# A router's layer norm with mean times deviation as a second operand from PSUM, interleaved with the next group's statistics

## The chip, the cores and the metric

One core of one Trainium2 chip. The metric is the device time of one execution in microseconds (us). Before the change three runs took 1918.94 us in the median (1918.43 to 1921.91).

## The reference, cut to what matters

The kernel computes a block of three layers on 8192 rows of 256 float32 values: `x = x + 0.5 * moe(norm(x))`, then `x = x + attention(norm(x))`, then `x = x + 0.5 * moe(norm(x))`. The change touches the norm in front of the two expert networks:

```python
def _layernorm(x, axis=-1, eps=1e-05):
    m = jnp.mean(x, axis=axis, keepdims=True)
    v = jnp.var(x, axis=axis, keepdims=True)
    return (x - m) / jnp.sqrt(v + eps)
```

Each expert network takes the normed rows, computes `logits = xf @ router_w.T` for 8 experts, a softmax, the top two of each row, and a list of at most 1280 rows for each expert; then every expert runs its rows through three matrices.

## The kernel before, in words

The 8192 rows are 64 tiles of 128 rows. All of x stays in SBUF (`xs`). Every expert network begins with a stage that this text calls **the norm stage** (`ffn_in` on each engine). It takes the tiles in 16 groups of four (G4 = 4); two groups are a pair, and 8 pairs are the 8 steps (STEPS = 8). Group q = 2i + r belongs to step i and to buffer r (0 or 1). Buffers `xn`, `rows`, `rstd`, `bst` and `mv` exist twice, once for each r.

For one group the work passes through the engines in this order:

- VectorE, `stats` (lines 920 to 930): four `bn_stats` (L924), four `bn_aggr` that write mean and variance into PSUM (`mv`, L928), and one small instruction that adds epsilon (L930). It releases `stat_ready`.
- GpSimd, `power` (L418): the power -1/2 of four numbers for each partition, giving `rstd`, which is one over the deviation. It releases `rstd_ready`.
- VectorE, `norm` (L937): four `tensor_scalar`, (x - mean) * rstd, each 128x256 float32 from SBUF to SBUF, with the two numbers for each partition as pointers (mean in PSUM, rstd in SBUF). It waits for `lo_ready` (the buffer of two groups ago is done with) and `rstd_ready`.
- ScalarE, `high` (L667): the upper float16 half of all four tiles into `rows`. It waits for the store of two groups ago and for `xn_ready`.
- GpSimd, `low` (L422): the lower half, `xn - high`, a `tensor_tensor` with two SBUF inputs and an SBUF output.
- TensorE transposes `rows` (L1346) into PSUM, ScalarE copies the result out (`turned`, L673), TensorE multiplies with the router's weights (L1357), and after every second group ScalarE takes the logits out (L677). SyncE stores `rows` to memory for the experts' gathers (L515) and, in the first network, loads the next pair of x (L518).

The engines' orders are written by hand. VectorE's before is, in step i: stats(i, 1), norm(i, 0), stats(i+1, 0), norm(i, 1). GpSimd's is power(2i+1), low(2i), power(2i+2), low(2i+1). ScalarE's is high(i, 0), the copies of the group before, the logits, high(i, 1), the copies. SyncE waits for the pair's load before, loads the next pair and then stores the two groups of this pair. Between the pieces of VectorE's order stands `beside(n)`, a hook. In the first network it holds three small router pieces (n = 0, 1, 2). In the second it holds the last work of the attention (`attention_end`): at n = 1 a residual sum (`finish`, L1198), at 4 to 10 a chain that builds the last batch's matrix together with TensorE and ScalarE (`m2_sums`, `m2_ctx`, `m2_out` L1240, `m2_top` L1247, `m2_scale` L250, `m2_lo`), and at 14, 16, 18, 20 four more residual sums. `ffn_in` runs some steps unrolled (1 in the first network, 5 in the second) and the others in a hardware loop. After the norm stage VectorE goes on with `top_two` (L971 to L996), GpSimd with constants, and the routing rounds follow.

Of the kernel before, what the change touches and what calls it, by code (L numbers as in the profile page):

```python
# [6 lines left out]
def macaron_block(nc, x, wq, bq, wv, bv, wo, bo, router_w, wg, wu, wd, out):  # L7
# [3 lines left out]
    add, sub, mult = ALU.add, ALU.subtract, ALU.mult  # L11


    P = 128
    B, SEQ, D = x.shape
# [17 lines left out]
    G4 = 4  # L33
    PAIR = 2 * G4
    STEPS = NT // PAIR
# [17 lines left out]
    with ctx:  # L53
        def sb(name, shape, dt):
            return ctx.enter_context(nc.sbuf_tensor(name, shape, dt))
# [4 lines left out]
        bank = [ctx.enter_context(nc.psum_tensor(f"bank{i}", [P, 512], f32)) for i in range(8)]  # L60
# [8 lines left out]
        xs = sb("xs", [P, NT, D], f32)  # L69
# [6 lines left out]
        xn = sb("xn", [P, 2, G4, D], f32)  # L76
        xt2 = sb("xt2", [P, 2, 2, 2 * KD, P], f16)
        bst = sb("bst", [P, 2, G4, 6], f32)
        mv = bank[1][:, 256:256 + 4 * G4].rearrange("p (r g s) -> p r g s", r=2, g=G4)
        rstd = sb("rstd", [P, 2, G4], f32)  # L80
        nmean = sb("nmean", [P, 2, G4], f32)
        ident16 = sb("ident16", [P, P], f16)
# [161 lines left out]
        def settle(eng):  # L244

            eng.sem_inc(s_passed, 1)
# [44 lines left out]
        def tiles(ap, t, n):  # L291

            return ap[:, t:t + n] if isinstance(t, int) else ap[:, bass.ds(t, n)]
# [554 lines left out]
        def _(dve):  # L848
# [69 lines left out]
            def ffn_in(S, ch, wait_x, head, beside):  # L918
                def stats(i, r):

                    t = i * PAIR + r * G4
                    wait_x(i, r)
                    for g in range(G4):
                        ch.mark(dve.bn_stats(bst[:, r, g, :], tiles(xs, t + g, 1)[:, 0]))  # L924
                    ch.wait()
                    settle(dve)
                    for g in range(G4):
                        ch.mark(dve.bn_aggr(mv[:, r, g, :], bst[:, r, g, :]))  # L928
                    ch.wait()
                    dve.tensor_scalar(rstd[:, r, :], mv[:, r, :, 1], EPS, XSCALE ** -2, add, mult).then_inc(S.stat_ready, 1)  # L930

                def norm(i, r):
                    t, q = i * PAIR + r * G4, 2 * i + r
                    dve.wait_ge(S.lo_ready, q + 1)
                    dve.wait_ge(S.rstd_ready, q + 1)
                    for g in range(G4):
                        last = dve.tensor_scalar(xn[:, r, g, :], tiles(xs, t + g, 1)[:, 0], mv[:, r, g, 0:1],  # L937
                                                 rstd[:, r, g:g + 1], sub, mult)
                    last.then_inc(S.xn_ready, 1)

                def step(i, beside):
                    stats(i, 1)
                    beside(4 * i + 1)
                    norm(i, 0)
                    beside(4 * i + 2)
                    stats(i + 1, 0)
                    beside(4 * i + 3)
                    norm(i, 1)
                    beside(4 * i + 4)

                stats(0, 0)
                beside(0)
                for i in range(head):
                    step(i, beside)
                with dve.Fori(head, STEPS - 1) as i:
                    ch.enter(i - head, 2 * 2 * G4)
                    step(i, nothing)
                    ch.leave(STEPS - 1 - head)
                stats(STEPS - 1, 1)
                norm(STEPS - 1, 0)  # L960
                norm(STEPS - 1, 1)

            def route(S, ch):

# [179 lines left out]
            def ffn(S, wait_x, head, beside):  # L1144
                ch = Chain(dve, S.dstep)
                ffn_in(S, ch, wait_x, head, beside)
                route(S, ch)
                for i in range(LP):
                    list_piece(S, 0, i)
                list_read(S, ch, 0)  # L1150
                for k in range(4):
                    dve.wait_ge(S.gu_hi, k + 1)
                    split_lo(k % 2, k // 2, S.gu_lo)
                with dve.Fori(0, E - 1) as e:
                    ch.enter(e, 3 + 1 + 3 + (0 if S.scaled else 12 + 4))
                    expert(S, ch, e, False)
                    ch.leave(E - 1)
                expert(S, ch, E - 1, True)

            ch = Chain(dve, at.dstep)  # L1160
# [451 lines left out]
```

## Time and profile before

| | |
|---|---|
| median of three runs | 1918.94 us |
| the profiled execution | 1917.76 us |
| its span, first to last instruction | 1916.0 us |
| TensorE busy | 1616.2 us (84% of the span) |
| VectorE busy | 1246.2 us (65%) |
| ScalarE busy | 887.6 us (46%) |
| GpSimd busy | 874.8 us (46%) |
| mean granted clock of TensorE | 0.943 |
| the norm stages | about 6 to 80 us and 1055 to 1135 us |

PE is TensorE, PEld its weight load, DVE VectorE, ACT ScalarE, POOL GpSimd, SP SyncE; a q behind the name is the engine's queue. Times count from the first instruction. In a timeline a row may hold several instructions in succession (x4): the second number is then the time from the start of the first to the end of the last. A busy share is not a bound: the norm stages use TensorE little, and what is worth something there is the chain of waits.

### The profile page before, as it was taken

How to read it: one execution, taken by the hardware profiler on the slowest of the kernel's cores; microseconds unless marked ns; L12 is line 12 of the kernel's file. 1: busy time of each engine (PE TensorE's matmuls, PEld its weight loads, DVE VectorE, ACT ScalarE, POOL GpSimd, SP SyncE). 2: the span in 40 equal slices, each digit the busy share in tenths (PEclk: the TensorE clock that was granted, in tenths of full speed). 3: DMA queues.
4: the chain of work that ended last, by engine and by line, in shares of the span. 5: the costliest groups of instructions: out<-in, count | busy, mean ns of one | idle time of the engine just before them, and what ended most of it. 6: DMA issues, size and time to landing. Idle time of an engine off the chain costs nothing.

```text
span 1916.0 us, 40317 instructions
## 1 busy us (share of the span) xinstructions
PE 1616.2 (84%) x13943; PEld 1275.8 (67%) x13943; DVE 1246.2 (65%) x2883; ACT 887.6 (46%) x1627; POOL 874.8 (46%) x636
## 2 busy tenths in 40 slices
PE   4512899999999999995899751289999999999998
PEld 3411687877878787773577641168787787878876
DVE  8987748576574856526898897763745546465551
ACT  4511445445454444535665551144544545445452
POOL 5623262644536354235776652326264452635423
PEclk9999999999999999996999755589999999999999
DMA  6650461614425152226766450045161442515212
GB/s 214 212 185 14 108 122 30 145 41 107 78 70 126 37 132 52 31 29 165 154 146 146 137 195 4 14 108 116 36 145 44 104 83 65 128 42 126 58 25 28
DMA packets 261236, 182.16 MB, mean 95 GB/s; under 512 B 160938, under 2 KB 247860, under 8 KB 261172
## 3 DMA queue, kind: packets, MB, share of 16 engines
q1 hardware_dynamic: 230452, 139.37, 26.7%
q0 software_dynamic: 30720, 41.96, 13.2%
q8 instruction: 36, 0.59, 0.1%
q14 instruction: 28, 0.23, 0.0%
HBM read 89.01 MB, written 54.53 MB: 75 GB/s over the span
## 4 chain that ended last, share of the span: by engine, by line
PE 72%; DVE 12%; issue 6%; POOL 5%; DMA 2%; ACT 2%; DVEq 0%; SPq 0%; POOLq 0%; ACTq 0%
PE bank L1439 43%; PE bank L1452 22%; PE bank L1420 3%; POOL rstd L418 1%; POOL rows L422 1%; DVE kT L1020 1%; DVE rT L1020 1%; PE bank L1400 1%; DVE gat L1229 1%; PE bank L1484 1%; ACT xn L778 1%; DMA xs<-in_L_attn_x 1%; POOL gat L395 1%; DVE xn L937 1%; DVE v L1223 1%
## 5 line engine op out<-in xcount | busy, mean ns | idle before, releaser
L1439 PE MATMUL bank<-xT,w_g 128*128 128x320 f16 x3072 | 503.1, 300 | 30.9 <-DMA xT<-gat 30.9
L1095 DVE SCALAR_TENSOR_TENSOR unit_buf<-bank,sc_cur,unit_buf 128x320 f32<-128x320 f32 x512 | 281.5, 550 | 353.9 <-PE bank L1439 227.9
L1439 PE MATMUL bank<-xT,w_u 128*128 128x320 f16 x3072 | 502.5, 300 | 0.0
L720 ACT ACTIVATE unit_buf<-bank,sc_cur 128x320 f32<-128x320 f32 x512 | 269.5, 526 | 407.1 <-PE bank L1439 405.6
L1452 PE MATMUL bank<-w_d,xs 128*128 128x256 f16 x3840 | 423.8, 273 | 0.0
L1452 PEld LDWEIGHTS bank<-w_d,xs 128*128 128x128 f16 x3840 | 375.2, 98 | 44.4
L1439 PEld LDWEIGHTS bank<-xT,w_g 128*128 128x128 f16 x3072 | 295.7, 99 | 141.0 <-issue 30.6
L389 POOL TENSOR_TENSOR hot_v<-hot_b,val 128x400 bf16<-128x400 bf16 x128 | 147.7, 1154 | 519.9 <-DVE hot_b L1078 519.9
L1439 PEld LDWEIGHTS bank<-xT,w_u 128*128 128x128 f16 x3072 | 301.3, 98 | 117.7
L1101 DVE TENSOR_TENSOR xs<-unit_buf,xs 128x320 f16<-128x320 f32 x512 | 268.0, 523 | 2.2
L395 POOL DMA_INDIRECT gat<-rows_d,id_next x160 | 177.0, 1106 | 200.4 <-DVE id_next L1088 140.0
L726 ACT ACTIVATE xs<-unit_buf 128x320 f16<-128x320 f32 x512 | 235.8, 461 | 10.4 <-DVE unit_buf L1095 10.4
L745 ACT ACTIVATE xs<-bank,w_fac 128x256 f32<-128x256 f32 x160 | 76.0, 475 | 277.4 <-PE bank L1452 276.3
L408 POOL DMA_INDIRECT out_x<-xs,id_cur x80 | 143.0, 1788 | 84.6 <-issue 76.1
L408 POOL DMA_INDIRECT x_d<-xs,id_cur x80 | 142.6, 1782 | 84.0 <-issue 73.6
L915 DVE SCALAR_TENSOR_TENSOR w_g<-raw_gu,sc_next,w_g 128x1024 f16<-128x1024 f32 x32 | 41.1, 1284 | 93.2 <-ACT w_g L661 93.2
L1420 PEld LDWEIGHTS bank<-hot_v,hot_a 128*128 128x128 bf16 x1024 | 82.3, 161 | 28.5 <-DVE hot_a L1080 24.3
L1420 PE MATMUL bank<-hot_v,hot_a 128*128 128x50 bf16 x1024 | 80.6, 219 | 22.2 <-POOL hot_v L389 22.2
L1400 PE MATMUL bank<-cnt,same_e 128*128 128x3 f32 x60 | 17.6, 363 | 95.7 <-DVE rT L1020 95.7
L422 POOL TENSOR_TENSOR rows<-xn,rows 128x1024 f16<-128x1024 f32 x32 | 68.4, 2136 | 45.2 <-ACT rows L667 45.2
L1080 DVE TENSOR_TENSOR hot_a<-pos_a,slot_a 128x1024 bf16<-128x1024 bf16 x128 | 87.3, 682 | 0.0
L1400 PEld LDWEIGHTS bank<-cnt,same_e 128*128 128x128 f32 x60 | 15.0, 310 | 98.9 <-DVE rT L1020 98.9
(229 smaller groups left out, 1815.2 us busy)
## 6 DMA issues: line engine op xcount, KB each, us to landing
rows_d<-rows SPq DMA_DIRECT2D x32, 512.0 KB, 3.4
raw_gu<-in_L_ffn_wg SPq DMA_DIRECT2D x16, 1024.0 KB, 6.3
raw_gu<-in_L_ffn_wu SPq DMA_DIRECT2D x16, 1024.0 KB, 9.3
raw_d<-in_L_ffn_wd SPq DMA_DIRECT2D x16, 1024.0 KB, 5.5
x_d<-xs SPq DMA_DIRECT2D x1, 8192.0 KB, 32.6
out_x<-xs SPq DMA_DIRECT2D x16, 512.0 KB, 3.7
xs<-in_L_attn_x SPq DMA_DIRECT2D x7, 1024.0 KB, 5.6
xs<-x_d SPq DMA_DIRECT2D x5, 1024.0 KB, 6.1
```

The costliest lines, as they stand in the source:

```text
L389: pool.tensor_tensor(hot_v[:, r], bc(hot_b[:, r], 2, 5), bc(vv, 3, ST), mult).then_inc(S.hot_v_ready, 1)
L395: pool.indirect_dma_start(out=gat[:, s, :], out_offset=None, in_=rows_d, in_offset=bass.IndirectOffsetOnAxis(ap=id_next[:, s:s + 1], axis= ...
L408: pool.indirect_dma_start(out=dst, out_offset=bass.IndirectOffsetOnAxis(ap=id_cur[:, s:s + 1], axis=0), in_=stage[:, s, :], in_offset=None ...
L422: pool.tensor_tensor(rows[:, r, :, D:2 * D], xn[:, r, :, :], rows[:, r, :, 0:D], sub).then_inc(S.lo_ready, 1)
L720: act.activation(act_s[:, u % 2, :], bank[u % 2][:, 0:CW], ACT.Silu, scale=sc_cur[:, 3:4]).then_inc(S.s_ready, 1)
L726: act.activation(hid[:, 0, f, c * CW:(c + 1) * CW], h32[:, u % HB, :], ACT.Copy).then_inc(S.hhi_ready, 1)
L1080: dve.tensor_tensor(hot_a[:, r], bc(pa, 1, P), slot_a[:, :, :], ALU.is_equal).then_inc(S.hot_a_ready, 1)
L1095: dve.scalar_tensor_tensor(h32[:, u % HB, :], bank[2 + u % 2][:, 0:CW], sc_cur[:, 4:5], act_s[:, u % 2, :], mult, mult).then_inc(S.h32_rea ...
L1101: dve.tensor_tensor(hid[:, 1, f, c * CW:(c + 1) * CW], h32[:, u % HB, :], hid[:, 0, f, c * CW:(c + 1) * CW], sub).then_inc(S.h_ready, 1)
L1420: last = pe.matmul(bank[6][:, 0:5 * ST], hot_a[:, i % 2, :, t], hot_v[:, i % 2, t].rearrange("p v s -> p (v s)"), start=(i == 0 and t == 0 ...
L1439: mm = pe.matmul(bank[2 * m + u % 2][:, 0:CW], wgu[m][:, w, k, f * P:(f + 1) * P], xT[:, a * KD + k, c * CW:(c + 1) * CW], start=(j == 0 a ...
L1452: mm = pe.matmul(bank[4 + s % 2][:, 0:D], hid[:, a, f, s * P:(s + 1) * P], wdn[:, w, f, :], start=(f == 0 and j == 0), stop=(f == FT - 1 a ...
```

## The change

The norm is now computed as x * rstd - (mean * rstd). A new small instruction (`means`) multiplies mean and rstd of a group into PSUM (`mean_r`), and `norm` is a `scalar_tensor_tensor`: in0 is the tile in SBUF, the scalar is rstd in SBUF, in1 is `mean_r` in PSUM, one number for each partition spread over 256 elements with step 0. `stats` is cut into `stats`, `moments` and `variance`, and a `turn` deals with one group: the statistics of the next group, `means` of this one, moments of the next, two tiles of the norm, variance of the next, two tiles. The hooks stand behind the turns, two after each.

```diff
--- before.py
+++ after.py
@@ -77,6 +77,7 @@
         xt2 = sb("xt2", [P, 2, 2, 2 * KD, P], f16)
         bst = sb("bst", [P, 2, G4, 6], f32)
         mv = bank[1][:, 256:256 + 4 * G4].rearrange("p (r g s) -> p r g s", r=2, g=G4)
+        mean_r = bank[1][:, 272:272 + 2 * G4].rearrange("p (r g) -> p r g", r=2)
         rstd = sb("rstd", [P, 2, G4], f32)
         nmean = sb("nmean", [P, 2, G4], f32)
         ident16 = sb("ident16", [P, P], f16)
@@ -922,43 +923,62 @@
                     wait_x(i, r)
                     for g in range(G4):
                         ch.mark(dve.bn_stats(bst[:, r, g, :], tiles(xs, t + g, 1)[:, 0]))
+
+                def moments(r):
                     ch.wait()
                     settle(dve)
                     for g in range(G4):
                         ch.mark(dve.bn_aggr(mv[:, r, g, :], bst[:, r, g, :]))
+
+                def variance(r):
                     ch.wait()
                     dve.tensor_scalar(rstd[:, r, :], mv[:, r, :, 1], EPS, XSCALE ** -2, add, mult).then_inc(S.stat_ready, 1)
 
-                def norm(i, r):
-                    t, q = i * PAIR + r * G4, 2 * i + r
-                    dve.wait_ge(S.lo_ready, q + 1)
-                    dve.wait_ge(S.rstd_ready, q + 1)
-                    for g in range(G4):
-                        last = dve.tensor_scalar(xn[:, r, g, :], tiles(xs, t + g, 1)[:, 0], mv[:, r, g, 0:1],
-                                                 rstd[:, r, g:g + 1], sub, mult)
-                    last.then_inc(S.xn_ready, 1)
+                def means(i, r):
+                    dve.wait_ge(S.rstd_ready, 2 * i + r + 1)
+                    ch.mark(dve.tensor_tensor(mean_r[:, r, :], mv[:, r, :, 0], rstd[:, r, :], mult))
+
+                def norm(i, r, tile):
+                    if tile == 0:
+                        dve.wait_ge(S.lo_ready, 2 * i + r + 1)
+                    ins = dve.scalar_tensor_tensor(xn[:, r, tile, :], tiles(xs, i * PAIR + r * G4 + tile, 1)[:, 0],
+                                                   rstd[:, r, tile:tile + 1],
+                                                   mean_r[:, r, tile:tile + 1].to_broadcast([P, D]), mult, sub)
+                    if tile == G4 - 1:
+                        ins.then_inc(S.xn_ready, 1)
+
+                def turn(i, r):
+                    n = r ^ 1
+                    stats(i + r, n)
+                    means(i, r)
+                    moments(n)
+                    norm(i, r, 0)
+                    norm(i, r, 1)
+                    variance(n)
+                    norm(i, r, 2)
+                    norm(i, r, 3)
 
                 def step(i, beside):
-                    stats(i, 1)
-                    beside(4 * i + 1)
-                    norm(i, 0)
-                    beside(4 * i + 2)
-                    stats(i + 1, 0)
-                    beside(4 * i + 3)
-                    norm(i, 1)
-                    beside(4 * i + 4)
+                    for r in range(2):
+                        turn(i, r)
+                        beside(4 * i + 2 * r + 1)
+                        beside(4 * i + 2 * r + 2)
 
                 stats(0, 0)
+                moments(0)
+                variance(0)
                 beside(0)
                 for i in range(head):
                     step(i, beside)
                 with dve.Fori(head, STEPS - 1) as i:
-                    ch.enter(i - head, 2 * 2 * G4)
+                    ch.enter(i - head, 2 * (2 * G4 + 1))
                     step(i, nothing)
                     ch.leave(STEPS - 1 - head)
-                stats(STEPS - 1, 1)
-                norm(STEPS - 1, 0)
-                norm(STEPS - 1, 1)
+                turn(STEPS - 1, 0)
+                means(STEPS - 1, 1)
+                ch.wait()
+                for tile in range(G4):
+                    norm(STEPS - 1, 1, tile)
 
             def route(S, ch):
```

## Rows read from the trace of the kernel before

**Rows 1.** The page: the chain that ended last, by engine.
```profile
PE 72%; DVE 12%; issue 6%; POOL 5%; DMA 2%; ACT 2%; DVEq 0%; SPq 0%; POOLq 0%; ACTq 0%
```

**Rows 2.** Waits, 28 to 72.5 us: waiter <- releaser, us in total, times, longest.
```profile
ACT rows L667 <- DVE xn L937: 11.0, 11, 1.5
```

**Rows 3.** Timeline, first network: start us, length us, engine, line, what, [idle before].
```profile
17.65 1.40 DVE L937 TENSOR_SCALAR xn<-xs,bank,rstd 128x256 f32<-128x256 f32 x4
...
37.96 2.13 POOL L422 TENSOR_TENSOR rows<-xn,rows 128x1024 f16<-128x1024 f32 x1 [1.12 <-ACT rows L667]
...
38.99 2.23 DVE L937 TENSOR_SCALAR xn<-xs,bank,rstd 128x256 f32 x4
...
41.14 1.39 DVE L924 BATCH_NORM_STATS2 bst<-xs 128x6 f32 x4
41.25 1.06 ACT L667 ACTIVATE rows<-xn 128x1024 f16<-128x1024 f32 x1 [1.54 <-DVE xn L937]
...
42.21 1.92 ACT L673 ACTIVATE xt<-bank 128x1024 f16<-128x1024 f16 x2
42.38 2.12 POOL L422 TENSOR_TENSOR rows<-xn,rows 128x1024 f16<-128x1024 f32 x1 [1.13 <-ACT rows L667]
42.68 0.39 DVE L928 BATCH_NORM_AGGREGATE bank<-bst 128x2 f32<-128x6 f32 x4 [0.15 <-DVE bst L924]
```

**Rows 4.** Single lines of VectorE: count, duration ns min/median/max, starts, shapes.
```profile
L937 DVE TENSOR_SCALAR xn<-xs,bank,rstd x4: 404/404/1245, 39.0 to 40.8; 128x256 f32 x4
...
L1229 DVE SCALAR_TENSOR_TENSOR gat<-gat,v x16: 1224/2006/2361, 890.6 to 1052.1; 128x1024 f32<-128x1024 f32 x16
...
L1198 DVE SCALAR_TENSOR_TENSOR xs<-bank,mx,xs x32: 732/739/752, 952.9 to 1109.7; 128x512 f32 x16, 128x512 f32<-128x512 f32 x16
...
L1240 DVE SCALAR_TENSOR_TENSOR t<-bank,zr,rT x8: 473/476/485, 939.7 to 1073.5; 128x256 f32<-128x256 f32 x8
```

**Rows 5.** Timeline of VectorE and GpSimd in the attention.
```profile
939.67 0.87 DVE L1240 SCALAR_TENSOR_TENSOR t<-bank,zr,rT 128x256 f32<-128x256 f32 x2 [1.30 <-PE bank L1533]
...
951.65 2.14 POOL L479 TENSOR_TENSOR unit_buf<-gat,unit_buf 128x1024 f16<-128x1024 f32 x1
...
952.87 1.41 DVE L1198 SCALAR_TENSOR_TENSOR xs<-bank,mx,xs 128x512 f32 x2
```

**Rows 6.** DMA issues, 14 to 80 us: count, KB each, median us to landing.
```profile
rows_d<-rows SPq DMA_DIRECT2D x14, 512.0 KB, 3.5
xs<-in_L_attn_x SPq DMA_DIRECT2D x6, 1024.0 KB, 5.6
```

**Rows 7.** Windows: stretch, length, busy us (and instructions) of each engine, clock, DMA share, GB/s.
```profile
41.30:50.10 8.80, 5.61 (x82) 4.80 (x81) 8.26 (x27) 6.04 (x8) 6.59 (x4) 1.00 0.73 237
```

**Rows 8.** Timeline, end of the first network's norm and start of its routing.
```profile
74.14 3.99 DVE L937 TENSOR_SCALAR xn<-xs,bank,rstd 128x256 f32<-128x256 f32 x8
...
76.68 1.06 ACT L667 ACTIVATE rows<-xn 128x1024 f16<-128x1024 f32 x1 [1.60 <-DVE xn L937]
...
81.48 2.12 POOL L422 TENSOR_TENSOR rows<-xn,rows 128x1024 f16<-128x1024 f32 x1 [1.36 <-ACT rows L667]
...
81.74 2.27 DVE L977 TENSOR_TENSOR t<-t,v 128x384 f32<-128x384 f32 x1
```

**Rows 9.** Timeline, norm of the second network's inputs.
```profile
1059.62 1.98 POOL L418 TENSOR_TENSOR rstd<-rstd,mhalf 128x4 f32<-128x4 f32 x2
...
1060.74 1.40 DVE L937 TENSOR_SCALAR xn<-xs,bank,rstd 128x256 f32<-128x256 f32 x4 [0.64 <-POOL rstd L418]
...
1077.41 0.28 DVE L1247 TENSOR_REDUCE m_top_s<-bank 1x1 f32<-1x128 f32 x1 [1.43 <-PE bank L1538]
...
1081.83 0.16 DVE L250 TENSOR_SCALAR mx<-bank 128x1 f32<-128x1 f32 x1 [2.10 <-PE bank L1542]
...
1109.05 1.40 DVE L1198 SCALAR_TENSOR_TENSOR xs<-bank,mx,xs 128x512 f32<-128x512 f32 x2
...
1129.27 4.00 DVE L937 TENSOR_SCALAR xn<-xs,bank,rstd 128x256 f32<-128x256 f32 x8
```

## The prediction

> **What bounds the kernel now.** I read the page's chain of waits first [rows 1]. TensorE holds 72% of it, nearly all in the experts, which the change doesn't touch. What can change lies in the two norm stages, so the chain inside these stages decides. The list of waits in the first of them shows one regular wait in front of ScalarE's `high`: 11 times, 11.0 us, on the norm [rows 2]. The timeline then shows the cycle [rows 3]. One `low` on GpSimd (L422) starts at 37.96, the next at 42.38, so a group takes 4.42 us. From the first group after the load (norm from 17.65, over at 19.05) to the end of group 14's norm at 76.68 [rows 8] it is 57.63 us for 13 groups, 4.43 each.
>
> The cycle's links can be read off in order [rows 3, 4]. A norm starts at 38.99, while `low` runs from 37.96 to 40.09. Its four instructions take 2.23 us, where the same four take 1.40 at 17.65 with no `low` beside them. The extra time lies in one instruction: 1245 ns against a median of 404, and it ends at 40.23, 0.14 after `low`. So the first `tensor_scalar` is held until `low` is over. Then come the other three (over at 41.22), `high` from 41.25 (1.06), and the next `low` from 42.38 (2.12), which holds the next norm. Norm's rest 1.13 + high 1.06 + low 2.12 + handovers 0.11 = 4.42. The cycle is closed by this hold, not by a semaphore: the norm waits only for the `low` of two groups ago.
>
> No engine is full: in 8.8 us (two groups) GpSimd works 6.59 and ScalarE 6.04, and VectorE's 8.26 hold some 1.7 us of being held [rows 7].
>
> The page "SBUF — State Buffer" of the Trainium skill, section "Who interferes with whom", says why: VectorE and GpSimd share a pair of ports, which a `tensor_scalar` from SBUF to SBUF can take whole, as can GpSimd, and the later one waits. By that rule the trace agrees (the 1245 ns).
>
> **The change part by part.**
>
> *The hold.* The new norm has one tensor in SBUF and one in PSUM. The nearest rows are L1198, also `scalar_tensor_tensor` with a PSUM tensor, an SBUF tensor and a pointer in SBUF: 32 of them lie between 732 and 752 ns, among them the pair at 952.87, right beside a GpSimd `tensor_tensor` of L422's kind (951.65 to 953.79) [rows 4, 5]. A `scalar_tensor_tensor` with both tensors in SBUF (L1229) spreads from 1224 to 2361 ns [rows 4]. So I take the hold as gone. With it the closed cycle is gone, and each engine has its own sum.
>
> *VectorE's sum for a group.* Statistics 1.39, aggregates 0.39 with 0.15 of waiting in front [rows 3]. The norm: L1240, the same instruction on 128x256 (PSUM and SBUF exchanged), takes 476 ns, and two in succession 0.87 us, so one follows the other after 0.39 [rows 4, 5]; four cost 1.57, where `tensor_scalar` costs (1.40 - 0.40)/3 = 0.33 each, 1.33. `means` isn't in the trace; it is a small operation like the variance's, and I estimate 0.16, all of it on the path, since the wait of `moments` now stands behind it too. Bounds: 0.08 (the step between two aggregates, (0.39 - 0.16)/3) and 0.32. The variance sits between two norm tiles: 0.10. Sum: 1.39 + 0.16 + 0.15 + 0.39 + 1.57 + 0.10 = 3.76; with the loop's branch I take **3.8 us** for 4.43. For the norm's step the bounds are 0.33 (today's) and 0.48 (nothing overlaps): 3.5 and 4.1 us.
>
> The page "VectorE: DVE Perf Modes" of the Trainium skill, section "The perf-mode tier table", speaks against the change: a float32 `tensor_scalar` within SBUF runs two elements a cycle, one with a PSUM operand one. By it 256 elements at 0.96 GHz would cost 0.13 us more for each tile, 0.53 a group, and the gain would be some 7 us smaller. The rows show 0.33 against 0.39, and my sum goes by them.
>
> *The other engines at 3.8 us.* GpSimd: `low` 2.12 + `power` about 1.0 (two in 1.98 [rows 9]) = 3.1. ScalarE: 1.06 + 1.92, with half a logits copy some 3.2. Both fit. Stores: `high` must wait until the store of two groups ago has landed, so two groups can't take less than `high` 1.06 + `low` 2.12 + landing 3.5 [rows 6] + handovers 0.3 = 7.0, 3.5 a group. The transfers are 0.73 busy in 8.8 us [rows 7], 6.4 us for each pair; at 7.6 us that is 0.85, so the landings may grow by half a microsecond, and the store's loop comes to about 3.75. It sits right beside VectorE's sum: SP's queue is the next in line, with a load of 5.6 us behind the stores. `power` of a group now starts behind the second norm tile, still 0.9 before the norm's end, and is over before `means` of the next turn asks for it.
>
> *First network.* Group 1 waits for its neighbour's load as before, but the new turn has the next group's moments inside: its norm ends about 0.35 later, at 19.4. Then 13 groups at 3.8 end group 14 at 68.8, against 76.68: **7.9 us**. The last two groups lose their joint norm [rows 8]: group 15 must now wait for `power`, and ends 2.7 instead of 1.5 us behind group 14. I cost this at nothing: routing's first instructions are held by `low` anyway, and L977 at 81.74 waits for the last `low` (81.48 to 83.60), whose start hangs on ScalarE's copies of group 14. If that cover is gone, it costs 1.2.
>
> *Second network.* `means` of group 0 waits for GpSimd's first `power`, which is late (1059.62) behind attention work; today only the norm waits (0.64 us at 1060.74) [rows 9]. Queued behind it are now the moments of group 1 and the residual sum L1198, which frees the PSUM bank that TensorE's chain needs. That costs about 1 us. The chain `m2_top`, `m2_scale` waits today 1.43 and 2.10 us for TensorE [rows 9]; the hooks in pairs put the first wait right behind its cause, the second behind a whole turn. I take that as even. From 1062 to the last residual sum at 1109.05 most groups aren't in the closed cycle, and I take 1 us of gain net. From there to the end of group 14 (1129.27 + 4.00 - 1.40 = 1131.87) it is 22.8 us; with 1.32 for the residual sum and five groups at 3.8, 20.3: 2.5 us. Together **3.5 us**.
>
> *Sum:* 7.9 + 3.5 = 11.4 us. The profiled execution, 1917.76, would be 1906.4; the median of the runs is 1.2 above it, so **1907.5 us**. With 3.5 us a group both terms rise to some 17 (1902); with 4.1 they fall to some 5 (1914).
>
> **The rivals.**
>
> *A new bound near the old one* (20%). The store's landing, the load, or a turn's waits hold the group at 4.15 us: 13 x 0.28 - 0.35 + 1.7 = 5 us, 1914 (1911.5 to 1916). For it: the transfers' 0.85, and a store's loop of 3.75 beside a sum of 3.76. Against it: two groups of slack in every buffer.
>
> *More than expected* (6%): norm steps at today's 0.33, and a shorter wait in the attention's chain: below 1902.
>
> *The hold remains* (6%), the case on the other side. The norm reads its pointer `rstd` from SBUF beside the tile; if this second read is held by `low` like L937's is, the cycle stays closed, and now has the dearer norm in it, 0.25, with the variance, 0.10. 4.43 becomes 4.8, over 28 groups 10 us: 1929. It decides from 4.45 us a group on. Against it stand the 32 even durations of L1198, which has such a pointer too.
>
> *The gain is swallowed* (4%): what follows the norm stage waits for something that doesn't come earlier, such as the first experts' weights or the stores. 1918. Against it: these loads are issued by SP behind the last `low`, so they move along.
>
> **How the numbers follow.** 64% for the forecast, 1902 to 1911.5. A measurement of this kernel can tell about 0.2% (3.8 us) from no change, so faster means below 1915.1. Forecast 64, high case 6 and 17 of the new bound's 20 make 0.87. Its other 3 and the swallowed 4 make 0.07, the remaining hold 0.06. The range from 1902 to 1915 holds the forecast and most of the new bound, about 8 in 10.
>
> **What would show it.** Each norm instruction at 0.47 to 0.49 us with no long one; `low` starting every 3.8 us; VectorE without gaps but for 0.15 in front of the aggregates; the end of group 14 near 68.8; the second stage shorter by 3.5. I am wrong if a norm instruction of over 1 us stays beside `low`, if ScalarE's `high` waits for the store, or if VectorE waits in `means` inside the loop.

## The result, and the profile after

The changed kernel takes 1909.69 us (median of five runs, 1907.42 to 1911.83) against 1918.94 before: a ratio of 0.9945 (0.9935 to 0.9956), 10.6 us faster by the ratio (the medians themselves differ by 9.3), where 11.4 were forecast. The profiled execution took 1911.83 us with a span of 1910.1, the slowest of the five.

On the page the chain by engine is the same as before within a percent [rows 1]:

```profile
PE 72%; DVE 12%; issue 6%; POOL 4%; DMA 2%; ACT 2%; SPq 0%; DVEq 0%; POOLq 0%; ACTq 0%
```

The new norm instruction in the whole trace (count, duration ns min/median/max, starts; it answers to L937 in [rows 4]):

```profile
L944 DVE SCALAR_TENSOR_TENSOR xn<-xs,rstd,bank x128: 444/472/480, 12.5 to 1126.9; 128x256 f32<-128x256 f32 x128
```

None of 128 is long. The hold is gone. A group of the first network that nothing hinders, on VectorE's timeline:

```profile
22.93 1.40 DVE L925 BATCH_NORM_STATS2 bst<-xs 128x6 f32 x4
...
24.25 0.15 DVE L939 TENSOR_TENSOR bank<-bank,rstd 128x4 f32<-128x4 f32 x1
24.56 0.39 DVE L931 BATCH_NORM_AGGREGATE bank<-bst 128x2 f32<-128x6 f32 x4 [0.15 <-DVE bank L939]
24.85 0.84 DVE L944 SCALAR_TENSOR_TENSOR xn<-xs,rstd,bank 128x256 f32<-128x256 f32 x2
25.61 0.15 DVE L935 TENSOR_SCALAR rstd<-bank 128x4 f32<-128x4 f32 x1
25.68 0.86 DVE L944 SCALAR_TENSOR_TENSOR xn<-xs,rstd,bank 128x256 f32<-128x256 f32 x2
26.46 1.40 DVE L925 BATCH_NORM_STATS2 bst<-xs 128x6 f32 x4
```

The count behind a row merges instructions in succession, and neighbours overlap, so read the starts, not the lengths: 1.32 for the statistics, 0.31 for the product, 0.29 for the aggregates, 0.76 and 0.78 for two tiles each, 0.07 for the variance: 3.53 us. That is VectorE's need. But the groups don't follow at 3.53. From 26.46 to the last statistics at 64.70 it is ten groups in 38.24 us, **3.82 each**, unevenly (3.5 to 4.3). The waits from 28 to 66 us (waiter <- releaser, us in total, times, longest) say on what:

```profile
POOL rows L423 <- ACT rows L668: 7.9, 10, 1.3
ACT rows L668 <- DMA rows_d<-rows: 5.4, 5, 1.5
...
DVE bank L939 <- POOL rstd L419: 1.3, 4, 0.7
```

and one instance in the timeline shows the order (L519 is the 1 MB load of x, L516 the stores):

```profile
39.52 0.40 SPq L519 DMA_DIRECT2D xs<-in_L_attn_x  x1
...
42.36 4.12 SPq L516 DMA_DIRECT2D rows_d<-rows  x2
...
46.94 1.06 ACT L668 ACTIVATE rows<-xn 128x1024 f16<-128x1024 f32 x1 [1.38 <-DMA rows_d<-rows]
...
48.08 2.13 POOL L423 TENSOR_TENSOR rows<-xn,rows 128x1024 f16<-128x1024 f32 x1 [1.18 <-ACT rows L668]
...
50.16 1.01 POOL L419 TENSOR_TENSOR rstd<-rstd,mhalf 128x4 f32<-128x4 f32 x1
...
51.20 0.17 DVE L939 TENSOR_TENSOR bank<-bank,rstd 128x4 f32<-128x4 f32 x1 [0.65 <-POOL rstd L419]
```

ScalarE's `high` is ready and waits for the store issued at 42.36, behind the load of 39.52, to land; `low` comes late; `power` stands behind it in GpSimd's order; and VectorE waits in `means`. Every second `high`, the one whose store is queued behind the 1 MB load, has this wait, and these start 7.2 to 8.3 us apart (31.29, 38.91, 46.94, 54.15, 62.48), 3.90 for a group. The `high` between them doesn't wait for a store, but stands in ScalarE's order behind the logits copy, which waits for TensorE; so VectorE waits in `means` for most groups. Worked out from its starts: the ten groups take 2.9 us more than VectorE's need, 2.2 of it in front of `means`, 0.4 once for a load of x (at 61.18), the rest in small gaps such as the loop's branch. The new bound is the cycle store, `high`, `low`, store.

The end of the first network's norm stage (answers to [rows 8]), 67.38 being the `low` of group 13 and 74.57 that of group 15:

```profile
67.38 2.13 POOL L423 TENSOR_TENSOR rows<-xn,rows 128x1024 f16<-128x1024 f32 x1 [0.67 <-ACT rows L668]
...
69.14 1.06 ACT L668 ACTIVATE rows<-xn 128x1024 f16<-128x1024 f32 x1
...
69.65 1.89 PE L1366 MATMUL bank<-ident,rows 128*128 128x128 f16 x16
...
70.51 0.17 DVE L939 TENSOR_TENSOR bank<-bank,rstd 128x4 f32<-128x4 f32 x1 [1.46 <-POOL rstd L419]
...
70.72 1.94 ACT L674 ACTIVATE xt<-bank 128x1024 f16<-128x1024 f16 x2 [0.52 <-PE bank L1366]
...
74.57 2.12 POOL L423 TENSOR_TENSOR rows<-xn,rows 128x1024 f16<-128x1024 f32 x1 [2.00 <-ACT rows L668]
```

and the start of the second's (to [rows 9]):

```profile
1056.98 0.17 DVE L939 TENSOR_TENSOR bank<-bank,rstd 128x4 f32<-128x4 f32 x1 [2.65 <-POOL rstd L419]
...
1058.43 0.86 DVE L944 SCALAR_TENSOR_TENSOR xn<-xs,rstd,bank 128x256 f32<-128x256 f32 x2
```

Where the time came from: the first comparison of the routing rounds starts at 94.38 instead of 101.29, 6.9 us earlier. In the second network, from the first statistics (1050.89, before 1054.57) to the copy in front of the rounds (1145.2, before 1152.2), it is 94.3 instead of 97.6, 3.3 us. Together 10.2. This one execution then gave 3.4 us away in the attention, with a granted TensorE clock of 0.69 from 855 to 950 us where before had 0.78. That isn't the change's: a later execution of the same kernel (below) doesn't have it, and one of the kernel before does (its third profile has the same 0.69 in this window, and an attention 5.1 us longer than in its first).

### The profile page after: what moved, and what is told of

The parts are those of the page before. It is cut to its first block, busy times and chain, and to the rows that moved or that the text cites. A ratio compares the mean times of both kernels' runs of the same rounds, so it can differ in the third digit from the quotient of the medians.

```text
span 1910.1 us, 40320 instructions
## 1 busy us (share of the span) xinstructions
PE 1622.9 (85%) x13943; PEld 1278.3 (67%) x13943; DVE 1231.0 (64%) x2915; ACT 886.9 (46%) x1627; POOL 869.0 (45%) x636
## 4 chain that ended last, share of the span: by engine, by line
PE 72%; DVE 12%; issue 6%; POOL 4%; DMA 2%; ACT 2%; SPq 0%; DVEq 0%; POOLq 0%; ACTq 0%
PE bank L1459 43%; PE bank L1472 22%; PE bank L1440 3%; POOL rstd L419 1%; DVE kT L1040 1%; DVE rT L1040 1%; POOL rows L423 1%; PE bank L1420 1%; PE bank L1504 1%; DVE gat L1249 1%; ACT xn L779 1%; DMA xs<-in_L_attn_x 1%; DVE v L1243 1%; DVE xn L944 1%; POOL hot_v L390 1%
## 5 line engine op out<-in xcount | busy, mean ns | idle before, releaser
L727 ACT ACTIVATE xs<-unit_buf 128x320 f16<-128x320 f32 x512 | 235.9, 461 | 10.6 <-DVE unit_buf L1115 10.6
L1420 PEld LDWEIGHTS bank<-cnt,same_e 128*128 128x128 f32 x60 | 15.0, 311 | 98.5 <-DVE rT L1040 98.5
```

The source lines that it names most:

```text
L727: act.activation(hid[:, 0, f, c * CW:(c + 1) * CW], h32[:, u % HB, :], ACT.Copy).then_inc(S.hhi_ready, 1)
```

## The experiments

Two theories at the start. **A**: the instruction's operands decide on the hold; with the hold gone the stores' landing sets the pace in the first network (3.82) and VectorE has 0.3 us of slack. **B**: the gain comes from the interleaving. The texts "Expected" were written before the runs and name further rivals C to I. For every kernel the table has the pace (mean of the last ten groups of the first network's norm stage, from the starts of their statistics), the start of the first routing comparison, and the second network's stage from its first statistics to the copy in front of the rounds. The ratio is against the kernel before on the same chip. The expectations count the first stage to the copy in front of the rounds, 2.8 us ahead of the first comparison (91.62 against 94.38 in the changed kernel, 98.5 against 101.3 before).

| kernel | median us | ratio (95%) | pace | first stage | second stage |
|---|---|---|---|---|---|
| before, first profile | 1918.94 | | 4.42 | 101.3 | 97.6 |
| changed, first profile | 1909.69 | 0.9945 (0.9935 to 0.9956) | 3.82 | 94.4 | 94.3 |
| changed again | 1980.09 | 0.9863 (0.9839 to 0.9887) | 3.83 | 93.8 | 93.1 |
| instruction alone | 1989.97 | 0.9904 (0.9884 to 0.9924) | 3.92 | 95.2 | 96.9 |
| order alone | 1999.02 | 0.9941 (0.9920 to 0.9963) | 4.49 | 102.9 | 99.0 |
| product in SBUF | 2007.66 | 0.9994 (0.9974 to 1.0013) | 4.83 | 107.5 | 103.2 |
| before again | 1919.60 | 0.9998 (0.9989 to 1.0007) | 4.42 | 101.0 | 97.7 |
| changed, third | 1906.70 | 0.9929 (0.9916 to 0.9942) | 3.82 | 93.9 | 94.5 |
| fifth bn_stats | 1910.23 | 0.9952 (0.9939 to 0.9965) | 3.85 | 94.6 | 97.0 |
| loads by group | 1904.93 | 0.9920 (0.9907 to 0.9933) | 3.66 | 90.9 | 93.3 |
| changed, fourth | 1982.18 | 0.9873 (0.9858 to 0.9887) | 3.94 | 94.9 | 93.7 |
| loads by group again | 1978.34 | 0.9863 (0.9843 to 0.9883) | 3.66 | 91.1 | 93.6 |
| and first turn in old order | 1981.16 | 0.9869 (0.9850 to 0.9889) | 3.66 | 91.2 | 93.4 |
| before, third | 1920.74 | 1.0002 (0.9990 to 1.0013) | 4.43 | 100.9 | 97.7 |

The rows from "changed again" to "product in SBUF" ran on one chip, the four from "before again" on a second, the three from "changed, fourth" on a third. On the first and the third of these chips the kernel before takes 86 to 89 us more than on the others, the changed kernel 70 to 75. The pace of 3.94 in "changed, fourth" holds one interval of 4.92 us, where a store's landing was waited for 2.2 us; the other nine average 3.83. The changed kernel's stages agree on all chips within 1.1 us (93.8 to 94.9) and 1.4 us (93.1 to 94.5), so the stages are what is compared here.

**The changed kernel again.**

> The changed kernel once more, beside the experiments. Theory A (the first network's groups follow at 3.82 us because the stores' landing closes the cycle; VectorE alone would need 3.52): the same 3.8 us a group, a ratio of 0.994 to 0.996. Its first profile showed the attention 3.4 us longer than before's with a granted TensorE clock of 0.69 instead of 0.78 from 855 to 950 us. If that belongs to the change, it is there again; if it is chance, the attention's length moves by some us from one execution to the next, and the total is 1907 to 1909.

Pace and stages repeat. The total doesn't: 1980 against 2008 on this chip. That is 27 us by the ratio, where the norm stages hold 12; the ratio expected (0.994 to 0.996) was missed. See the end of this section.

**The instruction alone**: the new norm and `means`, VectorE's order as before. In this and the following diffs `...` marks lines left out; where the number of marked instructions in a turn changes, the loop's count is adapted too, which isn't shown.

```diff
-                def turn(i, r):
-                    ...
+                def whole(i, r):
+                    stats(i, r)
+                    moments(r)
+                    variance(r)
+
+                def norms(i, r):
                     means(i, r)
-                    ...
+                    ch.wait()
+                    for tile in range(G4):
+                        norm(i, r, tile)
 
                 def step(i, beside):
-                    ...
+                    whole(i, 1)
+                    beside(4 * i + 1)
+                    norms(i, 0)
+                    beside(4 * i + 2)
+                    whole(i + 1, 0)
+                    beside(4 * i + 3)
+                    norms(i, 1)
+                    beside(4 * i + 4)
```

> The new instruction and the small product, in VectorE's order of before (statistics of a group whole, hooks as before). Theory A: the hold behind GpSimd's low is gone, since only the instruction decides on it; each norm instruction takes 0.47 us; with two waits exposed VectorE needs about 3.9 us a group, the stores' cycle 3.8, so 7 of the 7.6 us in the first network remain, total 1909 to 1912. Rival B (the gain is the interleaving's): a group stays at 4.4 us or above, 1917 to 1922.

The norm's line from 26 to 64 us in this kernel, and below it in the next two:

```profile
L944 DVE SCALAR_TENSOR_TENSOR xn<-xs,rstd,bank x40: 475/476/481, 25.8 to 62.3; 128x256 f32<-128x256 f32 x40
```

No long one, 3.92 us a group, 6.1 of the first stage's 6.9 us: theory A's numbers, and B falls. Against the changed kernel on the same chip the first stage is 1.4 us longer. In the second network only 0.7 of 3.3 us are left. There the order has its worth, together with the instruction: of the last four steps three take 3.5 to 3.7 us with it (the fourth, 4.6, again comes behind a store) and all four 3.8 to 4.0 without.

**The order alone**: the new turns with the old `tensor_scalar`, no product.

```diff
-                    ch.mark(dve.tensor_tensor(mean_r[:, r, :], mv[:, r, :, 0], rstd[:, r, :], mult))
...
-                    ins = dve.scalar_tensor_tensor(xn[:, r, tile, :], ...,
-                                                   rstd[:, r, tile:tile + 1],
-                                                   mean_r[:, r, tile:tile + 1].to_broadcast([P, D]), mult, sub)
+                    ins = dve.tensor_scalar(xn[:, r, tile, :], ...,
+                                            mv[:, r, tile, 0:1], rstd[:, r, tile:tile + 1], sub, mult)
```

> The new order with the old tensor_scalar (no product, mean as pointer). Theory A: the first norm instruction of a group is again held until low is over (over 1.2 us), the cycle is norm 1.13 + variance 0.1 + high 1.06 + low 2.12 + handovers 0.1 = 4.5 us a group, 1 to 3 us slower than before: 1919 to 1922. Rival B: 3.9 us a group or less, 1909 to 1912.

```profile
L943 DVE TENSOR_SCALAR xn<-xs,bank,rstd x36: 402/406/1815, 25.5 to 63.9; 128x256 f32 x36
```

The long ones are back, 4.49 us a group as worked out (4.5), and both stages are longer than before's by 1.6 and 1.4 us. The ratio of 0.9941 is not of the norm stages.

**The product in SBUF**: the changed kernel but for where `mean_r` lies.

```diff
-        mean_r = bank[1][:, 272:272 + 2 * G4].rearrange("p (r g) -> p r g", r=2)
+        mean_r = sb("mean_r", [P, 2, G4], f32)
```

> The changed kernel with the product's 8 numbers for each partition in SBUF instead of PSUM, so that the norm has two SBUF tensors. Theory A (two SBUF inputs meet low, which reads SBUF): the hold is back, now with the dearer instruction inside the closed cycle, 4.8 us a group, 1926 to 1930. Rival C (only the two-port mode of tensor_scalar met low, and a tensor with step 0 doesn't count as a second stream): 3.8 us a group as in the changed kernel, 1908 to 1911.

```profile
L944 DVE SCALAR_TENSOR_TENSOR xn<-xs,rstd,mean_r x32: 469/473/1755, 25.8 to 62.2; 128x256 f32<-128x256 f32 x32
```

The hold returns, up to 1755 ns, beside `low` as before's:

```profile
44.49 2.12 POOL L423 TENSOR_TENSOR rows<-xn,rows 128x1024 f16<-128x1024 f32 x1 [0.70 <-ACT rows L668]
...
45.14 2.15 DVE L944 SCALAR_TENSOR_TENSOR xn<-xs,rstd,mean_r 128x256 f32<-128x256 f32 x2
```

The first of the pair takes 1753 ns and ends at 46.89, 0.28 after `low`. A group takes 4.83 us, and the stages are 6.2 and 5.6 us longer than before's. Eight numbers for each partition, moved from PSUM to SBUF, cost 24 us in the two stages against the changed kernel on the same chip (13.7 and 10.1). By the page "SBUF — State Buffer" of the Trainium skill, section "Who interferes with whom", an instruction with two SBUF inputs meets a GpSimd instruction that reads SBUF; by that rule the trace agrees, and shows that a second tensor with step 0 counts.

**Before again, and the changed kernel a third time.**

> The kernel before, unchanged, for a profile on the chip of these runs. Theory D: on the chip of the first four experiments every kernel took some 65 to 90 us more, and all four stood 12 to 15 us lower against before than the norm stages of their profiles say, so what they share there is not the norm. If this kernel's profile has 98.5 us up to the routing rounds of the first network and 4.43 us a group on any chip, the norm stages are comparable between chips and the rest is the chip's. Ratio 1.000, group 4.43.

> The changed kernel for a third time, as the base of the next two. Theory A: 3.82 us a group in the first network, 91 to 92 us up to the routing rounds, ratio 0.994 on a chip like the first.

Before's stages are the same to 0.3 us in both profiles. The changed kernel's first stage is 7.1 and its second 3.2 us shorter, and the total 13.6 by the ratio. Its second network starts 7.7 us earlier than in this profile of before (1047.94 against 1055.61), not 3.7 as in the first profile: the attention's 3.4 us were that execution's.

**A fifth bn_stats** in each group, its result unused.

```diff
-        bst = sb("bst", [P, 2, G4, 6], f32)
+        bst = sb("bst", [P, 2, G4 + 1, 6], f32)
-                    for g in range(G4):
-                        ch.mark(dve.bn_stats(bst[:, r, g, :], tiles(xs, t + g, 1)[:, 0]))
+                    for g in range(G4 + 1):
+                        ch.mark(dve.bn_stats(bst[:, r, g, :], tiles(xs, t + g % G4, 1)[:, 0]))
```

> The changed kernel with a fifth bn_stats in each group, whose result nobody reads: 0.33 us more of VectorE's work a group. Theory A (the stores' landing sets the first network's pace and VectorE has 0.3 us of slack there, 3.52 against 3.82): 3.85 to 3.9 a group, the first network's stage longer by 0.5 to 1.5 us, the second's, where VectorE mostly sets the pace, by 3. Rival E (VectorE's sum is the bound, as the prediction had it, 3.76): 4.15 a group, the first stage longer by 4.3 us.

VectorE's timeline:

```profile
42.50 1.73 DVE L925 BATCH_NORM_STATS2 bst<-xs 128x6 f32 x5
...
46.35 1.72 DVE L925 BATCH_NORM_STATS2 bst<-xs 128x6 f32 x5
```

3.85 us a group, now even, since VectorE's need (3.53 + 0.33) is just above the stores' cycle. The 0.33 us, 13 times over, cost 0.7 us in the first stage and 2.5 in the second. So VectorE was not the bound in the first network, and mostly was in the second. Rival E's 4.15 is not there.

**Loads by group**: x comes in pieces of 512 KB, each in front of one store, with a semaphore for each parity. The diff shows the loop alone; in front of it the loads of groups 2 and 3 are cut in two as well.

```diff
-                    sp.wait_ge(S.loaded, 16 * i + 48)
-                    load_x(S.loaded, src_v, i + 2)
-                    store_rows(S, i)
+                    for b in range(2):
+                        sp.wait_ge(x_half[b], 16 * i + 32 + 48 * b)
+                        load_quad(x_half[b], src_v, 2 * i + 4 + b)
+                        store_group(S, i, b)
```

> The changed kernel with x loaded in pieces of one group (512 KB) between the stores, instead of 1 MB in front of two stores. Theory A (the store of an even group waits in the queue behind the 1 MB load, and its late landing holds ScalarE's high): the wait for rows_d goes, 3.55 to 3.65 a group, the first stage 2 to 3 us shorter than the changed kernel's. Rival F (the stores' landing is their own 3.5 us plus the shared bandwidth): 3.8 a group, no change.

ScalarE's waits from 28 to 66 us:

```profile
ACT rows L675 <- DMA rows_d<-rows: 2.2, 4, 0.7
```

On the same chip the changed kernel has 4.7 us here (5.4 in its first profile). The wait falls to 2.2 us, the pace to 3.66 (six groups at 3.52, later ones 3.5 and 3.9 in turn), and the first stage is 3.0 us shorter. Not all of this is the stores': 0.5 us is an earlier first statistics, and 0.8 a shorter wait for group 2's rows, which now hangs on a load of half the size; from group 2's statistics to group 15's it is 1.6. So the store behind the big load was the cause of more than half of the stores' wait. What is left has two parts, a wait for the stores (2.2 us) and this order:

```profile
47.96 0.32 ACT L685 ACTIVATE lg<-bank,rws 128x64 f32 x1 [0.68 <-PE bank L1383]
48.18 1.05 ACT L675 ACTIVATE rows<-xn 128x1024 f16<-128x1024 f32 x1
...
49.30 2.13 POOL L424 TENSOR_TENSOR rows<-xn,rows 128x1024 f16<-128x1024 f32 x1 [1.02 <-ACT rows L675]
...
52.43 0.17 DVE L946 TENSOR_TENSOR bank<-bank,rstd 128x4 f32<-128x4 f32 x1 [0.23 <-POOL rstd L420]
```

Here `high` (48.18) waits for no store, but comes behind the logits copy, which waits for TensorE. No run tells the two parts apart. Of the total, 1904.93 against 1906.70 has the right sign, but the intervals overlap.

**Once more on a third chip, and the second network's first turn in the old order.**

> The changed kernel, as the base of the two beside it: ratio 0.993 to 0.995, first network's stage 91 us, second network's 93 to 94.5 us from its first statistics to its routing rounds.

> Loads by group once more, to see whether its 2.9 us in the first stage show in the total: 88 us for the first stage, total 2 to 3 us below the changed kernel's.

```diff
+                def first_turn(beside):
+                    stats(0, 1)
+                    moments(1)
+                    variance(1)
+                    beside(1)
+                    means(0, 0)
+                    ch.wait()
+                    for tile in range(G4):
+                        norm(0, 0, tile)
```

> Loads by group, and in the second network the first turn alone in the old order: group 1's moments and variance and the residual sum stand ahead of the product that waits for GpSimd's late first power. Theory G (the late power costs the changed kernel 0.8 us there, as the end of group 0's norm moved from 7.6 to 8.4 us after the first statistics): group 1's power starts 4 us earlier, the second stage is 0.5 to 1.5 us shorter than 93.3. Rival H (the attention's chain behind it waits for TensorE anyway): the second stage stays at 93.3 within 0.3.

Loads by group gain 3.8 us in the first stage, of which 1.1 is the one long interval of the changed kernel on this chip; the total's 1978.34 against 1982.18 says the same, again within overlapping intervals. The first turn in the old order gives nothing that can be told: 93.4 against 93.6, where one kernel's second stage moves by up to 1.4 us. Group 1's `power` starts 1.7 us earlier after the first statistics, not the 4 expected, and the statistics of the fourth group 1.8 us earlier (15.5 instead of 17.3). At the sixteenth 0.2 of that is left (68.6 instead of 68.8). That fits rival H: the 0.8 us that group 0 comes late are waited out further on.

**What stays open: 12 to 16 us on two chips.** The four kernels on the first of them stand 27, 19, 12 and 1 us under before by the ratio. By their norm stages the first two should stand 12.0 and 6.8 under it, the other two 3.0 and 11.8 above. Left over are 12 to 16 us, in kernels that share the changed kernel's code but not its effect. In their profiles TensorE stands still in the experts with no releaser, as in the waits of "changed again":

```profile
PE bank L1472 <- issue: 18.5, 28, 2.4
```

In the profiles from the other chips this row isn't there. A profile of before on such a chip is missing; its third is from a chip of the other kind:

> The kernel before once more. On two of the chips so far every kernel took 60 to 90 us more than on the others, TensorE stands still for some 45 us between matmuls of the experts without a releaser, and the changed kernel is 24 to 27 us below before instead of 9 to 13. Theory I: on such a chip before's norm stages are as on the others (98.5 us to the first routing rounds, 97.7 in the second network), and the 12 to 15 us that are left over lie in its experts, as more of this standing still than the changed kernel has. If this run falls on a chip of the other kind, it shows only that before is at 1918 to 1920 there.

Its stages are those of before (100.9 and 97.7). Whether before stands still longer there, and why, was not shown.

## Why the prediction was right, step by step

**The closed cycle and its hold: right, and shown.** The first instruction's 1245 ns are gone from 128 norms; with the old instruction in the new order they are back, and with the second tensor in SBUF too. That it is the second tensor and not a pointer is shown as well: all 128 have the pointer `rstd` in SBUF, and none is held. The two paces, 4.49 and 4.83, are what the same sum of links gives for these cases (4.5, worked out ahead of that run, and 4.8, the prediction's for the rival in which the hold remains). That rival was priced at 10 us slower; measured by the stages with the product in SBUF it is 11.8. Its own condition, a pointer's read that is held, didn't come about.

**The sum for VectorE: mis-sized.** The step "statistics 1.39 + product 0.16 + wait 0.15 + aggregates 0.39 + norm 1.57 + variance 0.10 = 3.76" put the lengths of the statistics and the aggregates end to end where instructions overlap; by starts it is 3.53 (0.07 less for the statistics, 0.10 for the aggregates, 0.06 for norm and variance). The instruction's own cost was right: 0.47 long, 0.38 from one to the next, forecast 0.39. By the page "VectorE: DVE Perf Modes" of the Trainium skill, section "The perf-mode tier table", a tile would cost an estimated 0.13 us more. The trace doesn't agree: it shows 0.05 to 0.06.

**The bound: the wrong one of two near ones.** Of the three signs of being wrong that the prediction named, two came: ScalarE's `high` waits for the store (5 times, 5.4 us), and VectorE waits in `means` inside the loop (up to 0.7 us). The forecast of 3.8 us a group came out at 3.82, but not as VectorE's sum: the stores' cycle, which the prediction had at 3.75 "right beside", holds the groups. The fifth bn_stats and the loads by group show it from both sides. That the number came out was luck: two estimates 0.01 apart stood next to each other, the one that was used 0.2 too high, the other about right. Had the stores landed sooner, the groups could have followed nearer to 3.5, as six of them do with the smaller loads, and the gain would have been larger than forecast.

**First network.** Group 14's norm ends at 69.04; forecast was 68.8, before 76.65. The step "I cost this at nothing" for the last two groups failed by 0.7 us: of 7.6 us, 6.9 arrive at the routing. The cover was thought to be ScalarE's copies behind group 14's `high`. But `low` of group 13 moved only from 73.33 (the row of before is below) to 67.38, 5.95 us, since it runs behind a late `high`; so its transposes on TensorE are now last (the copies wait 0.52 for them). Group 15's norm ends 3.3 us behind group 14's, where 2.7 were forecast, since its `power` too stands behind that `low`.

```profile
73.33 2.12 POOL L422 TENSOR_TENSOR rows<-xn,rows 128x1024 f16<-128x1024 f32 x1 [1.12 <-ACT rows L667]
```

**Second network.** Group 0's norm ends 8.40 us after the first statistics instead of 7.57, 0.8 where 1 was forecast. Up to the last residual sum it is 52.86 instead of 54.48 us, 1.6 where 1 was forecast; from there to group 14's end 20.2 instead of 22.8, the 2.5 forecast. The tail costs 0.9 again. In all 3.3, forecast 3.5.

**The sum.** 11.4 forecast, 10.2 by the two stages, 10.6 by the ratio, 9.3 by the medians. On the other chip of this kind the same kernel gained 10.3 by the stages and 13.6 by the ratio.

## What to carry to other kernels

When a GpSimd instruction and a VectorE instruction run side by side, look for the one long instance in a group of equal ones and for an end that falls on the other engine's end. A small operand in PSUM instead of SBUF can lift such a hold, at a dearer instruction, and pays where the hold closes a cycle. Sum an engine's need by starts, not by lengths, and when two bounds come out alike, test which holds before tuning either: here 0.33 us more work on VectorE in every group cost 0.7 us in one stage, and smaller loads in front of the stores, which touch no engine, shortened it by 3 us.

## What was not expected

Chips differ by more than this change: before takes 1919 us on some and 2007 on others, where the changed kernel's norm stages stay as they are, and its lead is 25 to 27 us instead of 11 to 14. And one profiled execution can lose 3.4 us in a stage that the change doesn't touch, so the gain was counted stage by stage.
